# A batch of eight blocks of x cut into two of four, with its scales ahead in GpSimd's order

## The reference

```
xn = layernorm(x)
xn2 = layernorm(xn) * gamma + beta
v, x1, x2 = split(xn2 @ W_in + b_in)
y = causal_conv(causal_conv(v, k0) * x1, k1) * x2      # 128 taps for each channel
attn = xn + y @ W_out + b_out
ffn = (silu(xn @ w_gate.T) * (xn @ w_up.T)) @ w_down.T # integer weights, scaled by 1/127
out = x + attn + ffn
```

## Time and profile before

| | |
|---|---|
| median of 3 runs | 339.22 us (339.11 to 339.55) |
| the profiled execution, its time | 339.5 us |
| its span in the profile | 336.4 us |
| mean granted TensorE clock | 0.981 |
| PE, DVE, ACT, POOL busy | 304.7, 248.3, 178.1, 213.2 us |

### The profile page before, as it was taken

How to read it: one execution, slowest core, us unless ns; L and a number is a source line. 1 busy time by engine, 2 the same in 40 slices (tenths; PEclk the granted TensorE clock), 3 DMA queues, 4 the chain that set the end, 5 groups by cost and what they waited for, 6 DMA issues and landing times.

```text
span 336.4 us, 11840 instructions
## 1 busy us (share of the span) xinstructions
PE 304.7 (91%) x4945; PEld 238.0 (71%) x4945; DVE 248.3 (74%) x512; ACT 178.1 (53%) x373; POOL 213.2 (63%) x292
## 2 busy tenths in 40 slices
PE   0859898988899999999999999999999999989993
PEld 0348677976667777787777877777777867558982
DVE  2689999864485775695576679678666777979994
ACT  3737996744343544434444444453544534479991
POOL 6799879267878888677785868867777662200000
PEclk9967999999999999999999999999999999999998
DMA  7992043167869678796787868778687888101345
GB/s 225 343 365 67 7 146 165 38 249 272 351 220 380 229 289 311 262 376 218 329 304 275 366 229 336 276 282 348 241 362 256 299 351 312 46 0 65 126 149 168
DMA packets 21505, 81.01 MB, mean 241 GB/s; under 512 B 1478, under 2 KB 12618, under 8 KB 13258
## 3 DMA queue, kind: packets, MB, share of 16 engines
q1 hardware_dynamic: 19458, 77.47, 62.2%
q0 software_dynamic: 1840, 2.36, 2.4%
q10 hardware_dynamic: 152, 0.40, 0.5%
HBM read 75.50 MB, written 4.72 MB: 238 GB/s over the span
## 4 chain that ended last, share of the span: by engine, by line
PE 48%; DVE 20%; ACT 11%; POOL 10%; issue 7%; DMA 2%; POOLq 0%; DVEq 0%; SPq 0%; ACTq 0%
PE bank_c L300 13%; PE bank_p L300 9%; PE bank_u L300 8%; PE bank_g L300 8%; PE bank_d L300 8%; ACT vx L764 3%; DVE hhl L985 3%; ACT vx L756 3%; DVE sgh L980 3%; POOL ybuf L1292 2%; POOL res L1235 2%; DMA bands<-in_L_attn_W_in 2%; ACT hhl L694 2%; POOL res L1236 2%; DVE stats L796 2%
## 5 line engine op out<-in xcount | busy, mean ns | idle before, releaser
L300 PE MATMUL bank_d<-wd,hhl 128*128 128x256 f16 x384 | 84.3, 271 | 0.3 <-DVE hhl L985 0.2
L300 PEld LDWEIGHTS bank_p<-wq,xT 128*128 128x128 f16 x1536 | 70.6, 99 | 17.0 <-issue 2.8
L300 PE MATMUL bank_p<-wq,xT 128*128 128x64 f16 x1536 | 80.0, 194 | 2.6 <-DVE wq L877 2.6
L300 PEld LDWEIGHTS bank_c<-ybuf,bands 128*128 128x128 f16 x1024 | 51.4, 96 | 21.6 <-issue 5.0
L300 PE MATMUL bank_u<-xT,wgu 128*128 128x512 f16 x192 | 66.2, 378 | 0.4 <-DVE sgh L980 0.4
L300 PE MATMUL bank_g<-xT,wgu 128*128 128x512 f16 x192 | 66.2, 377 | 0.0
L300 PE MATMUL bank_c<-ybuf,bands 128*128 128x64 f16 (+3 forms) x1024 | 60.2, 184 | 4.3 <-DVE ybuf L1005 4.3
L300 PEld LDWEIGHTS bank_c<-vhl,bands 128*128 128x128 f16 x1024 | 49.0, 96 | 18.8 <-issue 3.5
L300 PE MATMUL bank_c<-vhl,bands 128*128 128x64 f16 (+3 forms) x1024 | 57.3, 184 | 2.4 <-DVE x1y L824 1.2
L694 ACT CAST hhl<-sgh 128x512 f16<-128x512 f32 x48 | 29.7, 619 | 47.3 <-DVE sgh L980 47.3
L1195 POOL TENSOR_TENSOR vx<-vx,bias 128x512 f32<-128x512 f32 x32 | 37.8, 1183 | 25.8 <-DVE vx L837 25.8
(11 more groups left out here) (191 smaller groups left out, 553.2 us busy)
## 6 DMA issues: line engine op xcount, KB each, us to landing
bands<-taps_seq SPq DMA_DIRECT2D x64, 1024.0 KB, 8.1
out<-res SPq DMA_DIRECT2D x8, 512.0 KB, 3.0
res<-in_L_attn_x SPq DMA_DIRECT2D x3, 1024.0 KB, 16.2
res<-in_L_attn_x SPq DMA_DIRECT2D x2, 512.0 KB, 6.1
bands<-in_L_attn_W_in SPq DMA_DIRECT2D x1, 768.0 KB, 6.5
bands<-in_L_ffn_w_gate POOLq DMA_DIRECT2D x1, 768.0 KB, 11.0
bands<-in_L_ffn_w_up POOLq DMA_DIRECT2D x1, 768.0 KB, 14.0
vx<-in_L_ffn_w_down POOLq DMA_DIRECT2D x1, 768.0 KB, 16.0
```

The source lines that it names most:

```text
L300: return nc.tensor.matmul(o, w, m, start=start, stop=stop, skip_group_check=True)
```

## The change

The batch of blocks 8 to 15 becomes two, 8 to 11 and 12 to 15. SP issues the load of 12 to 15 behind the four loads of the taps. POOL makes the first set of scales for 8 to 11 ahead of the second set for blocks 0 to 3; the first set for 12 to 15 comes at b = 4, followed there by the second set for 4 to 7. The second set for 8 to 11 stays at b = 9, and that for 12 to 15 goes to b = 14.

```
-    CUTS = (0, 4, 8, 16, 24, NB)
+    CUTS = (0, 4, 8, 12, 16, 24, NB)
...
-    SCALES_1, SCALES_2 = (4, 14, 22), (9, 20, 27)
+    SCALES_1, SCALES_2 = (4, 14, 22), (4, 9, 14, 20, 27)
...
             load_x(3)
             load_x(4)
+            load_x(5)
...
             split_input_weights()
+            first_scales(2)
             second_scales(0)
-            second_scales(1)
             for b in range(4, NB + LX + 2):
                 if b in SCALES_1:
-                    first_scales(SCALES_1.index(b) + 2)
+                    first_scales(SCALES_1.index(b) + 3)
                 if b + 2 < NB and NORM[b + 2] == "P":
                     normalise(b + 2)
                 if b in SCALES_2:
-                    second_scales(SCALES_2.index(b) + 2)
+                    second_scales(SCALES_2.index(b) + 1)
```

## The result

| | kernel before | changed kernel |
|---|---|---|
| median of 8 runs each | 339.17 us (338.51 to 339.77) | 341.39 us (340.74 to 343.11) |
| ratio, 95% interval | | 1.0073 [1.0054, 1.0092] |
| the profiled execution: time, span | 339.5, 336.4 us | 342.77, 341.2 us |

The change makes the kernel slower by 2.2 us. The prediction was 339.8 with 341.0 as its upper end: the sign of the forecast was right, the size was not, and the time lies outside the range. Two terms failed: what VectorE and POOL were to give back (0.3 us), and the ends of the program, which were taken as unchanged. Two more matmuls on TensorE alone make the program end late.

What follows compares the result with a forecast made beforehand. It took a chain of waits through VectorE to TensorE at 43.85, without slack behind it, as the bound. A loss of 0.9 us there, partly given back, left +0.6: 339.22 + 0.6 = 339.8 us, range 338.6 to 341.0.

Steps and rivals of the forecast that it cites:

- The early wait: Ahead of block 6, TensorE waits 1.3 us for residual scales of blocks 0 to 3; VectorE keeps 0.3 of 0.66 us.
- POOL's prices: On POOL, each four-block scales call costs 2.0 us, plus 0.63 once beside VectorE's split of the input weights.
- The transfers: Loading x of blocks 12 to 15 behind the taps' loads costs 0; a later VectorE wait would absorb 0.5 us.
- Block 17 and the maxima: Scales of 12 to 15 delay block 17's transpose 1.1 us, the matmul of the maxima 1.0, taken as 0.9.
- What gives some back: At 52.09, VectorE's one-column operation beside POOL's add_bias waits less, so 0.9 us of lateness shrinks to 0.6.
- The third rival: Slower, nothing absorbed: L902 still waits its full time and 0.9 to 1.2 us come through, 340.3; chance 0.15.
- 3.1 lie around it; both stay: The profiled execution took 339.5 us, its span 336.4; the 3.1 us around the span were taken as unchanged.
- The fourth rival: TensorE's clock falls after gaps before blocks 16 and 17, costing 1.7 to 5 us, 342; chance 0.08.

Runs made afterwards that it cites:

- the second order of the calls: Changed kernel with POOL's second scales of blocks 0 to 3 ahead of the first scales of 8 to 11: 342.04 us, ratio 1.0073.
- the last comparison: The changed kernel, unaltered, run beside three other kernels on one chip, against the kernel before: 341.28 us, ratio 1.008.
- second profiled execution: The kernel before, unaltered, profiled once more to see how far the first 20 us vary: 339.9 us.

## Why the prediction was wrong

1. *The early wait.* Forecast 24.3 for the small matmul ahead of block 6 and 28.95 for block 7's split; measured 24.14 and 28.85, in an execution whose projections start 0.3 us early. Right within that, by the forecast steps. That the two then about balance fits the run that removed this wait alone and won nothing.
2. *POOL's prices.* Forecast 2.0 us for a call of four; the rows give 1.91 from 39.42 to 41.33. The operation beside the weights' split took 0.88, forecast 0.84. VectorE's split had begun first (21.29, POOL's operation at 21.40) and took 0.94 us as before, so POOL paid and VectorE did not. Right. The transfers cost 0 as forecast: VectorE's wait for x at 23.60 took 0.88 us, before 0.76.
3. *Block 17 and the maxima.* Forecast 42.1 and 44.85, taken as 0.9 late; measured 42.05 and 44.71, 0.86 late. Right. The sum left out that VectorE's diagonal (L965) would take 0.29 instead of 0.98 us; that was worth only the 0.26 of TensorE's idle time (last section), which the cautious 0.9 happened to cover.
4. *"What gives some back" failed.* I let VectorE reach the last statistics 0.5 us late, "since it isn't held by TensorE throughout", and L902 shrink. POOL's call for blocks 24 to 31, which follows these statistics, came 1.15 us late, and L903 took 0.90 as before. Where TensorE waits for POOL, ScalarE and VectorE wait for TensorE, and the whole front moves. On top of this POOL made TensorE wait once more, ahead of block 22 (6 below): the lateness is 0.86 at the matmul of the maxima, 1.05 at block 22's small matmul, 1.12 at the bands' transposes of 58.04, and 1.10 (332.89 - 331.79) at the last VectorE instruction, instead of 0.6. The third rival, nothing absorbed, is what happened there, by a path that it did not name.
5. *"3.1 lie around it; both stay" failed.* I took the time around the computations as constant. Of the changed kernel 341.02 - 339.4 = 1.6 us lie outside the span instead of 3.1, but 339.4 - 332.89 = 6.5 instead of 336.4 - 331.79 = 4.6 us of the span lie behind the last VectorE instruction. Both together are 0.7 us more on the mean of all executions, since two more matmuls make TensorE's last event about 2 us late. No step of the prediction looked at the ends of the programs. With this term right, the measured 341.39 us would have been some 340.7, inside the range; with step 4 right and this one wrong, some 340.9 by the two traces. It took both to leave it.
6. *What was not seen:* block 22's small matmul. Before, POOL's second scales of 16 to 23 ended at 46.25, 0.77 us before TensorE came to use them at 47.02. The timelines of POOL and TensorE before:

```profile
44.58 1.67 POOL L1180 TENSOR_TENSOR lns<-lns,minus_half 128x8 f32<-128x8 f32 x1
```

```profile
47.02 0.29 PE L300 MATMUL bank_u<-lns,hhl 128*128 128x8 f32 x2
```

   In the changed kernel they end at 46.26 + 1.67 = 47.93, 1.68 us later, and the matmul starts 0.14 us behind that, as in the two runs with the late call at b = 15 (0.14 and 0.13 us). By TensorE's own row ahead of it (47.12, before 46.36) it would have started at 47.78: TensorE waited 0.3 us for POOL, though the view shows no bracket for it. The two cuts add 2 x 1.93 - 2.73 = 1.13 and 2 x 1.91 - 2.57 = 1.25 us to POOL; 0.62 of it goes into the idle time at 36.5 (0.96 to 0.34), and 1.7 us come through, of which the 0.77 of slack at block 22 takes a part. I priced single waits where the engine behind all of them was full, so a repair of either wait looked worth more than it is.
7. *The fourth rival* was a real mechanism and not this change's: it came with the second order of the calls.

The sum after the fact: 1.10 at the last VectorE instruction and 0.7 behind it are 1.8 us, of 2.2 (first comparison) and 2.6 (last one) in the medians. The profiled execution of the kernel before, 339.5 us, was itself 0.2 to 0.8 us above the medians of that kernel (338.7 to 339.3). The spans on record say where: in the last comparison their medians are 335.95 us for the kernel before and 339.65 for the changed one, while the two traces have 336.4 and 339.4. Less the 4.6 and 6.5 us that lie behind the last VectorE instruction in the traces, the medians are 1.8 us apart there (an estimate), where the traces show 1.10. So in the median some 1.8 us come before that point and 0.7 behind it, and step 4 was off by more than the two traces say. Which rows make the difference of 0.7 between median and traces is open.

No version is clearly faster than the kernel before. The nearest are the kernel before with the second scales of 0 to 7 in one call (338.23) and the cut with everything behind the first scales joined again (338.18, against 338.71 in its comparison); both intervals just include 1. Both have the second scales of 0 to 7 in one call, and the cut adds nothing to that which can be measured.

## What to carry to other kernels

Before pricing the waits that a change removes or adds, sum what it adds to the engine that all of them wait for, and set that against this engine's idle time ahead of the next common point; if it exceeds it, reordering only moves the wait. Splitting a batch costs a fixed part per call on each engine that handles it, here over a microsecond for each pair of calls on GpSimd, and a long wait of another engine (6.2 us on ScalarE) is no reason to pay it. Compare also what lies behind the last computation, engine by engine: a program that is two instructions longer can end later.

## What the runs showed of the hardware

*The end of TensorE's program.* With 4947 matmuls TensorE's last event comes 1.6 to 2.2 us behind the other engines', with 4945 it coincides, whatever else is changed. "Runtime: NRT & Kernel Launch", section "Instruction fetch mechanics", of the Trainium skill says that an engine takes its program in blocks of 16 KiB (256 instructions), which it fetches by itself, and that crossing into another block is mostly hidden. The traces have such transfers: queue 8 carries 41 packets of 16,384 bytes, room for 10,496 instructions by that figure of the Trainium skill, and only TensorE's program is that long (10,145 of its instructions are in the trace of the kernel before). In the rows of the last run the last of these packets moves from 337.12 to 338.08 us, and TensorE's last event comes 1.28 us behind it. So it is in all 10 traces with 4947 matmuls (1.22 to 1.35 us behind the packet's end), while in all 8 with 4945 TensorE's last event comes 0.3 to 0.9 us before that packet's end and so does not wait for it. This fits a border of blocks that the two matmuls push ahead of the last event, and it is not hidden here. No run moved the border in single steps, so this cause is argued from the times of the packets; the effect of the two matmuls alone is shown.

*The start.* TensorE's small matmuls of 384 columns in the first 20 us run at two speeds, though the profile shows a granted clock of 1.00 in both: 0.91 us for a merged pair in the kernel before, 1.64 in its second profiled execution. Timelines of TensorE, first the kernel before, then that second execution:

```profile
16.09 0.91 PE L300 MATMUL bank_p<-vhl,ones 1*128 1x384 f32 x2
```

```profile
18.69 1.64 PE L300 MATMUL bank_p<-vhl,ones 1*128 1x384 f32 x2
```

The reading of 1.00 can't be taken at its word there. The pair of transposes at 23.35 takes 0.67 us in the kernel before, at a granted clock of 0.50. The same pair takes 0.67 in the second execution too, at a shown clock of 1.00, and a later pair 0.42. Timeline of TensorE of that second execution:

```profile
25.73 0.67 PE L324 MATMUL bank_g<-ident,ybuf 128*128 128x128 f32 x2
...
33.20 0.42 PE L324 MATMUL bank_u<-ident,ybuf 128*128 128x128 f32 x2
```

By the durations TensorE ran at the lower level in that execution from 14 us at the latest until some 32 us, while in the first one the matmuls between about 14 and 20 us had the full rate. This is how the same program comes to end its preparatory matmuls 3.3 us late (20.33 against 17.00). From 20 to 30 us both are at the lower level, and the late one loses nothing more: 2.4 us are left at the first projections (25.00 against 22.63) and 1.0 at the end. A comparison of two timelines needs a point where both agree before it says anything.

*POOL and VectorE beside each other.* POOL's four-column product took 0.88 us beside VectorE's split of the weights and 0.20 elsewhere, in this order as in the one before (0.84). VectorE's diagonal (L965 before, L966 now) took 0.98 us from 42.82 beside POOL's add of the bias, an operation with two tensor inputs that ended at 43.71, and 0.29 from 43.58 in the changed kernel beside a normalisation, which has one. In all 12 traces in which the diagonal starts beside that add it ends 0.1 us behind the add, whatever its own length (0.59 to 1.05 us), so VectorE waited for POOL's operation to end. The 0.7 us that VectorE wins there gave TensorE only its 0.26 us of idle time ahead of the maxima.
